# A two-layer decoder on one core: expert weight rows fetched by broadcast transfers, semaphores cleared earlier, and a GELU in halves

## The reference, cut to what matters

```python
x = x + L0_attn(layernorm(x))          # stage A, 16 heads of 64, scores refined by a small MLP
x = x + L0_xattn(layernorm(x), ctx)    # stage B
x = x + L0_ffn(layernorm(x))           # stage C
x = x + L1_attn(layernorm(x))          # stage D
x = x + L1_xattn(layernorm(x), ctx)    # stage E, masked
x = x + L1_ffn(layernorm(x))           # stage F, mixture of experts
```

```python
combined = concat([scores, kerple])                 # per query and key: 32 values
hdn = gelu(combined @ w1 + b1, approximate=False)
scores = scores + kerple + (hdn @ w2 + b2)          # then causal softmax, values, output product
```

```python
g = silu(h @ w_gate[e].T); u = h @ w_up[e].T        # h: 512 tokens x 256, 128 hidden features
routed = sum_e (g * u * combine[:, e]) @ w_down[e].T
out = routed + shared(h)
```

## Time and profile before

| | us |
|---|---|
| median of three runs (4124.12 to 4130.19) | 4125.24 |
| the profiled execution's own time | 4128.32 |
| its span, first to last instruction | 4126.5 |
| L1232 PE, x1088, mean of one | 0.598 |
| L1245 PE, x128, median of one | 0.382 |
| L1682 ACT, GELU of 128x2048, median of one | 1.97 |
| DVE idle ahead of L1716, behind L1584 | 218.7 |

### The profile page before, as it was taken

How to read it: one execution, slowest core, us unless ns; L and a number is a source line. 1 busy time by engine, 2 the same in 40 slices (tenths; PEclk the granted TensorE clock), 3 DMA queues, 4 the chain that set the end, 5 groups by cost and what they waited for, 6 DMA issues and landing times.

```text
span 4126.5 us, 59377 instructions
## 1 busy us (share of the span) xinstructions
PE 3815.9 (92%) x22610; PEld 1837.7 (45%) x22610; DVE 2427.9 (59%) x6081; ACT 1740.2 (42%) x3188; POOL 152.0 (4%) x168
## 2 busy tenths in 40 slices
PE   4899899999989989999998998999999999899999
PEld 2353444345435244435543524443553443444355
DVE  5568576832466856673236676766323776676542
ACT  1655434521274643362127464336113836433511
POOL 1000020000000002000000001100000000200000
PEclk9999999999999999999999999999999999999999
DMA  5313002122331200203242210120325121012031
GB/s 174 122 43 63 19 18 54 22 96 73 102 109 43 55 19 25 57 12 104 72 127 93 43 38 18 45 48 1 115 62 162 63 51 26 19 45 48 1 126 55
DMA packets 135286, 254.49 MB, mean 62 GB/s; under 512 B 23332, under 2 KB 82724, under 8 KB 130084
## 3 DMA queue, kind: packets, MB, share of 16 engines
q1 hardware_dynamic: 134984, 250.50, 21.7%
HBM read 156.04 MB, written 44.04 MB: 48 GB/s over the span
## 4 chain that ended last, share of the span: by engine, by line
PE 74%; DVE 16%; ACT 7%; issue 2%; PEldq 0%; SPq 0%; DMA 0%; PEld 0%; DVEq 0%; POOLq 0%; ACTq 0%
PE ps L1232 11%; PE ps L588 7%; PE ps L571 6%; PE ps L1250 5%; DVE mx L754 4%; PE ps L411 4%; PE ps L515 4%; PE ps L1604 3%; PE ps L1520 3%; PE ps L576 3%; ACT a_X L1682 2%; PE ps L467 2%; PE ps L1544 2%; DVE ps L751 2%; PE ps L1563 2%
## 5 line engine op out<-in xcount | busy, mean ns | idle before, releaser
L692 ACT ACTIVATE PT<-ps 128x512 f32<-128x512 f32 (+2 forms) x1280 | 644.2, 564 | 325.2 <-PE ps L576 174.7
L1232 PE MATMUL ps<-xnT,f_w 128*128 128x512 f32 x1088 | 493.8, 598 | 0.0
L754 DVE TENSOR_REDUCE mx<-ps 128x1 f32<-128x512 f32 (+3 forms) x768 | 431.1, 618 | 76.4 <-PE ps L515 39.6
L571 PE MATMUL ps<-QS,KS 99*128 99x512 bf16 (+2 forms) x1280 | 419.1, 369 | 8.5 <-ACT PT L692 8.0
L515 PE MATMUL ps<-KS,QS 96*128 96x512 bf16 (+3 forms) x1280 | 392.2, 368 | 17.4 <-DVE mx L754 6.9
L751 DVE CUSTOM_DVE_ANT_0 ps<-ps,mneg 128x512 f32<-128x512 f32 x512 | 340.8, 718 | 82.0 <-PE ps L515 78.9
L1338 DVE TENSOR_TENSOR f_tm<-f_si,ps 128x512 f32<-128x512 f32 x128 | 88.1, 688 | 492.1 <-ACT f_si L1290 492.0
L588 PE MATMUL ps<-PT,VP 128*32 128x512 f32 (+3 forms) x2560 | 372.0, 573 | 0.0
L411 PE MATMUL ps<-mneg,identb 128*128 128x512 bf16 x1192 | 312.9, 389 | 28.5 <-DVE a_fin L1716 10.5
L1290 ACT ACTIVATE f_si<-ps 128x512 f32<-128x512 f32 x136 | 80.8, 597 | 595.5 <-PE ps L1245 576.4
L1232 PEld LDWEIGHTS ps<-xnT,f_w 128*128 128x128 f32 x1088 | 208.6, 193 | 206.5 <-issue 199.9
(11 more groups left out here) (278 smaller groups left out, 5524.1 us busy)
## 6 DMA issues: line engine op xcount, KB each, us to landing
f_w<-in_wF SPq DMA_DIRECT2D x136, 384.0 KB, 3.1
scores<-a_fin SPq DMA_DIRECT2D x64, 256.0 KB, 3.0
a_fin<-scores SPq DMA_DIRECT2D x32, 512.0 KB, 4.5
a_Y<-in_wA SPq DMA_DIRECT2D x5, 3072.0 KB, 15.1
KS<-KP SPq DMA_DIRECT2D x240, 64.0 KB, 2.3
scores<-a_fin SPq DMA_DIRECT2D x64, 192.0 KB, 2.9
a_fin<-scores SPq DMA_DIRECT2D x12, 1024.0 KB, 7.6
a_fin<-scores SPq DMA_DIRECT2D x16, 768.0 KB, 4.3
```

What stands on the lines that cost most here:

```text
L571: last = nc.tensor.matmul(o, m["KS"][0:KST, h, j * P:(j + 1) * P], m["QS"][0:KST, h, q0:S], start=True, stop=plain)
L692: nc.scalar.activation(m["PT"][:, mp % 2, j % 2, e, 0:w], ps[:, SLOTS + n % TURNED, 0:w], ACT.Exp, scale=HD ** -0.5).then_inc(g("exp"), 1)
L754: nc.vector.tensor_reduce(m["mx"][:, h % 2, i, f // BANK:f // BANK + 1], ps[:, k % SLOTS, 0:w], AX.X, ALU.max, negate=True).then_inc(g("sl ...
L1232: last = nc.tensor.matmul(ps[:, 2 * v + e % 2, :], m["w"][:, e % NRING, (2 * v + k) * P:(2 * v + k + 1) * P], xnT[:, k, :], start=(k == 0) ...
```

## The change

Three parts. **Rows of weights.** `routed(e)` remains for e = 2 and 3 (`F_DIRECT`). For the other 30 a new product `all_rows` brings all 32 rows out once, as 32 partitions of 512 tokens; ACT copies them to `f_rows` (`rows_up`), SP stores them in DRAM (`weight_rows`, 64 KB) and then fetches row after row, each broadcast to 128 partitions (2 KB each, 256 KB together), into four slots in `ctxT`, two experts behind the transfers of expert weights on the same queue. DVE's second product reads the row there. The transposition of the weights moves into the middle of up(3). **Border.** SP clears most semaphores ahead of F's barrier, issues `out<-x` behind the second barrier instead of ahead of it, and `WARM_CLEAR` is 8. **GELU in halves.** In the 16 units of two-unit chunks the GELU is two instructions of two banks each. In the second unit of such a chunk, up(k) starts with four of its products behind the first half.

```diff
-WARM_ROUND, WARM_CLEAR = 12, 6
+WARM_ROUND, WARM_CLEAR = 12, 8
+F_ROWS = 4
+        row_in = [setup_loaded, setup_dve, setup_pool_sem, setup_act]
+        F_DIRECT = [NSH, NSH + 1]
+        rows_kept = nc.dram_tensor("weight_rows", (NE, S), F32, kind="Internal").ap()
+        def row_of(e):
+            return ctxT[:, e % F_ROWS // 2, e % 2 * S:(e % 2 + 1) * S]
@@ f_sp
+            def load_row(e):
+                if e > F_DIRECT[-1] + F_ROWS:
+                    sp.wait_ge(sm["F", "gu"], e - F_ROWS + 1)
+                sp.dma_start(row_of(e), rows_kept[e - NSH:e - NSH + 1, :].partition_broadcast(P)).then_inc(row_in[e % F_ROWS], 16)
+            lag = 2
+            first = F_DIRECT[-1] + 1
             for e in range(NE + NSH):
+                if e == first + lag + F_ROWS - 2:
+                    sp.wait_ge(sm["F", "rows_up"], 1)
+                    sp.dma_start(rows_kept, MF["rows"][:, :]).then_inc(sm["F", "rows_out"], 16)
+                    sp.wait_ge(sm["F", "rows_out"], 16)
+                    load_row(first)
+                    load_row(first + 1)
                 if e >= NRING:
                     sp.wait_ge(sm["F", "down"], e - NRING + 1)
                 sp.dma_start(MF["w"][:, e % NRING, :], io["wF"][e]).then_inc(w_in[e % NRING], 16)
...
+                if e >= first + lag + F_ROWS - 2:
+                    load_row(e - lag)
+            for e in range(NE + NSH - lag, NE + NSH):
+                load_row(e)
@@ f_pe
+                half_up(e, 0)
+                if e == F_DIRECT[-1]:
+                    weights_turned()
+                half_up(e, 1).then_inc(g("gu_mm"), 1)
...
+            def all_rows():
+                nc.tensor.matmul(ps[0:NE, 5, :], selE[:, :, 0], m["cT"][:, :], start=True, stop=True).then_inc(g("rows_mm"), 1)
...
             up(NSH + 1)
+            pe.wait_ge(g("ct_up"), 1)
             routed(NSH)
-            routed(NSH + 1)
+            all_rows()
             down(NSH)
...
-                routed(e)
+                if e - 1 in F_DIRECT:
+                    pe.wait_ge(g("rows_up"), 1)
+                    routed(e - 1)
                 down(e - 1)
@@ f_dve
+                    if e in F_DIRECT:
+                        dve.wait_ge(g("row_mm"), e - NSH + 1)
+                        row = ps[:, 4 + e % 2, :]
+                    else:
+                        dve.wait_ge(row_in[e % F_ROWS], 16 * ((e - F_DIRECT[-1] - 1) // F_ROWS + 1))
+                        row = row_of(e)
+                    nc.vector.tensor_tensor(m["gu"][:, e % 2, :], m["tm"][:, :], row, ALU.mult).then_inc(g("gu"), 1)
@@ a_pe
+                tiles = list(itertools.product(range(4), range(2)))
+                if k == FIRST[c]:
...
+                else:
+                    pe.wait_ge(g("gelu"), HIDDEN_TO[k] - 1)
+                    for e, b in tiles[:4]:
+                        scored(e, b)
+                    pe.wait_ge(g("gelu"), HIDDEN_TO[k])
+                    for (e, b), (e2, b2) in zip(tiles[:4], tiles[4:]):
+                        scored(e2, b2)
+                        last = distant(e, b, 0)
+                    last.then_inc(g("w1"), 1)
+                    for e, b in tiles[4:]:
+                        last = distant(e, b, 0)
+                    last.then_inc(g("w1"), 1)
@@ a_act
-                act.wait_ge(g("w1"), k + 1)
                 if k >= 2:
                     act.wait_ge(g("w2"), k - 1)
-                nc.scalar.activation(m["hid"][k % 2][:, :, 0:w], ps[:, A_UP:A_UP + 4, 0:w], ACT.Gelu, bias=b1A[:, 0:1]).then_inc(g("gelu"), 1)
+                n = 4 // HALVES[k]
+                for x in range(HALVES[k]):
+                    act.wait_ge(g("w1"), HIDDEN_TO[k] + x + 1)
+                    nc.scalar.activation(m["hid"][k % 2][:, n * x:n * x + n, 0:w], ps[:, A_UP + n * x:A_UP + n * x + n, 0:w], ACT.Gelu,
+                                         bias=b1A[:, 0:1]).then_inc(g("gelu"), 1)
@@ sync
+                    if s == STAGES[-1]:
+                        clear_all(sp, done_by_now)
                     st.end()
...
+                st.end_round([s for s in counting if s not in done_by_now])
                 sp.dma_start(out[bass.ds(b, 1), :, :].rearrange("o (t p) d -> p (o t) d", p=P), x[:, :, :]).then_inc(x_stored, 16)
-                st.end_round(counting)
```

More of the change, by code:

```diff
@@ L1191, in f_mem @@
             m["cT"] = sb2("f_cT", [96, S], BF16)
+            m["rows"] = sb2("f_rows", [NE, S])
             m["si"] = sb2("f_si", [P, 2, S])
@@ L1224, in f_pe, with half_up @@
             last.then_inc(g("lg_mm"), 1)
+            def half_up(e, v):
+                for k in range(KD):
+                    last = nc.tensor.matmul(ps[:, 2 * v + e % 2, :], m["w"][:, e % NRING, (2 * v + k) * P:(2 * v + k + 1) * P],
+                                            xnT[:, k, :], start=(k == 0), stop=(k == KD - 1))
+                return last
             def up(e):
@@ L1427, in decoder @@
         TILE_END = {i: max(n for n in range(NCHUNK) if CHUNKS[n][0] == i) for i in range(NI)}
+        HALVES = [2 if FIRST[c] != LAST[c] else 1 for c, _ in A_UNITS]
+        HIDDEN_TO = [sum(HALVES[:k]) for k in range(NU + 1)]
         V_HEADS = [4, 2, 1, 1]
@@ L1556, in up, with scored @@
                     pe.wait_ge(g(loaded(c)), 16 if c >= SMALL else 16 * (c // 4 + 1))
-                if k:
-                    pe.wait_ge(g("gelu"), k)
-                for e in range(4):
+                def scored(e, b):
                     rows = slice(32 * e, 32 * e + 32)
-                    for b in range(2):
-                        first = (q0 + b * R) * L
-                        nc.tensor.matmul(ps[64 * b:64 * b + 64, A_UP + e, 0:R * L], w1A[rows, 0, :], fin(c)[rows, first:first + R * L],
-                                         start=True, stop=False, tile_position=(32 * e, 64 * b), skip_group_check=True)
@@ L1565, in up @@
-                for q in range(R):
-                    for e in range(4):
-                        rows = slice(32 * e, 32 * e + 32)
-                        for b in range(2):
-                            t0 = BACK - i * P - AU * (r + q0 + b * R + q)
-                            last = nc.tensor.matmul(ps[64 * b:64 * b + 64, A_UP + e, q * L:(q + 1) * L], w1A[rows, 1, :], kerA[rows, t0:t0 + L],
-                                                    start=False, stop=True, tile_position=(32 * e, 64 * b), skip_group_check=True)
@@ L1577, in down @@
                 w = SA_R[i] * L
-                pe.wait_ge(g("gelu"), k + 1)
+                pe.wait_ge(g("gelu"), HIDDEN_TO[k + 1])
                 if k:
@@ L1911, in _ @@
             st.end_round(counting)
+            done_by_now = [ctx_loaded, *x_biased.values(), *w_loaded.values(), *(a for (stage, _), a in sm.items() if stage != STAGES[-1])]
             with sp.Fori(0, rounds) as b:
```

46 lines of the change are left out of this document (29 added, 17 removed).

## The result

Time after: 4089.64 us median of four executions (4084.67 to 4095.34), before 4124.68 (4123.81 to 4130.19); ratio 0.9913, 95% interval [0.9896, 0.993]. The forecast was 4082.5, in a range of 4068 to 4098. The profiled executions stand at 4128.32 and 4084.67, 43.6 apart against 42.7 in the sum; the medians are only 35.0 apart. The profiled execution after was the fastest of the four, and its mean granted clock was 0.987 against 0.984 to 0.985 in the others. Both have to be explained, the 43.6 and the 8 or so that the medians lack. The latter are hardly clear of noise: as a ratio the forecast was 0.9898, just inside the measured interval. The median also lies above the forecast's own range of 4076 to 4088, where rivals (a) and (b) had put theirs (4090.5 and 4089), so the number alone doesn't tell which mechanism held.

The account below looks back on a forecast made before the run. PE was taken to bound the kernel, with 74% of the chain. Stage F -39.1, stage A -6.8, border +1.3 and program's end +1.9 sum to -42.7 us, giving 4082.5 us, range 4068 to 4098.

Parts of the forecast that it names:

- (a): F's start: the clock stays low, giving back 4 x 2.0 us, 4090.5 in all; chance 0.13.
- (b): Stage A gives nothing, extra batches and DVE waits take all: 4089, or 4093 with a loss; chance 0.15.
- 29 products at 0.22: Stage F, steady part: experts 5 to 33 lose their row product on PE, 6.4 us a round.
- (d): Stage F: the row broadcast is served at the upper bound of 8.8 us, about 4470 in all; chance 0.04.
- down(2) starts at 898.29 ... 1.73 and 3.43 lead to 903.45: F's start: down(2) after 0.55 of waiting, then down and up; part of a 3.4 us gain a round.
- the 0.83 that the prediction gave to the slow clock at down(2): F's start: down(2) took 2.56 instead of 1.73 at the low clock; full clock was assumed after the change.
- 1.7 a round: Stage A: net gain of halved GELUs after the cost of extra batches, 6.8 us in all.
- The half GELU's 1.11: Stage A: a half GELU takes 1.11 us by slope, two in a row 0.14 more than the whole.
- the last two second units cost 0.7 each: Stage A: second units 13 and 15 lie where PE bounds, so each extra batch costs 0.7 us.
- -1.5 to +2: Border: range in us, each, for the change in the unexplained 3.87 us way back to the loop's head.
- (c): Stage A or border does better: way back shorter by 1.5 or batches of four overlap; about 4072, chance 0.16.
- it was 3.1 slower than the median ... against that I forecast: Whole kernel: profiled execution 4128.3 was 3.1 above the median 4125.2, so 4085.6 there became 4082.5 us.

Follow-up runs that it names:

- e4_fill: Changed kernel with two idle products ahead of down(2) and three ahead of down(3) at F's start; 4090.5 us, ratio to before 0.9907.
- e5_border_6: Kernel before with semaphores cleared earlier and the store of out behind the second barrier, idle products still six; 4135.8 us, ratio 1.0022.
- e10_whole_late: Changed kernel with the border of before and a whole GELU and one batch of eight in second units from 12 on; 4086.1 us, ratio to before 0.9902.
- e2_halves: Kernel before with only the GELU in halves, stage F and border unchanged; 4123.9 us, ratio 0.9991.
- e6_only_8: Kernel before with eight idle products at the border instead of six and nothing else; 4136.3 us, ratio 1.0023.
- e3_border: Kernel before with only the border changed: earlier clears, store of out behind the second barrier, eight idle products; 4140.3 us, ratio 1.0029.

## Why the prediction was right, and where it was not

**F, steady: right in mechanism and size.** 29 products at 0.22 were 6.38 a round, 25.5 in all. The broadcast landed after 3.4 us, beside the 3.1 taken from the expert transfer, and rival (d) was not near: its limit was put where row and expert transfer together exceed 5.16 us, and two rows with an expert's weights still did not. Issue to landing is not service time; the earlier trace rows had said so with their 1.0 us between two landings.

**F, start: the step "down(2) starts at 898.29 ... 1.73 and 3.43 lead to 903.45" was short.** It gave 2.66 a round instead of 3.4. Both waits were near the forecast, but a down behind a wait for its own stationary operand takes 1.99, not 1.73: in the steady part the first weight load starts 0.43 us ahead of its product, under the up, behind a wait it starts together with it. Twice 0.26, and 0.2 in the hand-overs. Rival (a) is refuted: 1.00 in the earlier trace rows's place after, 13.27 in all rounds of the seven other kernels profiled with this order, and no effect of `e4_fill`. The old order's low clock was in turn no certainty: in 2 of the 20 rounds profiled with it up(3) to up(5) took 14.23, not 15.93, as in round 2 of `e5_border_6`:

```profile
1911.60:1916.60 5.00, 3.09 (x12) 2.01 (x11) 2.75 (x4) 1.08 (x2) 0.00 (x0) 1.00 0.00 0
1916.60:1921.60 5.00, 5.00 (x18) 2.98 (x17) 1.28 (x2) 0.60 (x1) 0.00 (x0) 1.00 0.26 79
```

The chain of that round has the same down(2) and up(4), for the 2.56 and 4.56 of the earlier trace rows:

```profile
1913.92 1.99 PE ps L1250 x8
1915.91 3.43 PE ps L1232 x8
```

So 0.26 of the 0.83 that the prediction gave to the slow clock at down(2) were the bare weight load, which stayed. The clock was worth 1.7 of the 2.66, and the new order 0.96.

**A: 1.7 a round was near, by two errors.** The half GELU's 1.11 was right (1106 ns). Of the gains, up(5) is 1.9 earlier behind the first up and up(11) 2.9. But "the last two second units cost 0.7 each" was wrong: `e10_whole_late` finds at most 0.15. That a split up costs so little I put down to its middle, where products of both halves stand in turn; no run tested that. Up to the weighted sums 139 us behind the first up the gain is 2.3. Then half of it goes in 5 us, by the clock: the windows there after and, at the same instructions, before:

```profile
1272.20:1277.20 5.00, 5.00 (x19) 3.93 (x20) 2.46 (x10) 0.00 (x0) 0.00 (x0) 0.74 0.13 51
```
```profile
1289.90:1294.90 5.00, 4.93 (x28) 3.96 (x30) 3.24 (x13) 0.00 (x0) 0.00 (x0) 1.00 0.15 61
```

This low is no accident of one round: the six us from 136 us behind the first up ran at 0.72 to 0.75 in all 36 rounds with halves, and at 1.00 in the seven rounds of 167.4 to 167.7 with a whole GELU. Rounds 2 to 4 keep 1.1; round 1 shows 5.5, because there the kernel before was 4.2 above its other rounds. Rival (b), that A gives nothing, is refuted for A itself; in the median, `e2_halves` says 2.5 us of the 6.8.

**Border: mis-sized.** The drain grew by the forecast 0.43 (1.82 for 1.39), and the way back by 0.3 (4.19 for 3.87), which was inside "-1.5 to +2". It goes with the store's new place and the earlier clears, which no run separates, and not with the idle products: three ways back took 12.5 to 13.0 us in the traces of the six kernels with the new order, `e5_border_6` and its six products among them, and 11.8 to 12.1 in the other eight, also in `e6_only_8`. The earlier clearing gave nothing, as said. The end of the program cost the 1.9. So rival (c), a shorter way back, is refuted. What the prediction had no term for is what a shift of the rounds does behind the border. It priced two idle products at 1.3; alone on the kernel before they cost 10.

**The sum for the profiled execution: near by luck.** The rows of the first table add up to -43.7 where the forecast had -42.7. F gave 3.0 less than forecast and the borders and the end cost 1.0 more; against that stand 1.9 more in A, all of it and more from one bad round of the kernel before, and 3.1 in stretches for which the forecast had nothing.

**The median: the failed step is "it was 3.1 slower than the median ... against that I forecast".** It carries a sum made for one execution over to the medians, as if the executions of both kernels stood alike in their clock. But the profiled execution before was 3.1 above its median and the one after 5.0 below. The kernel before was the steadier of the two: 18 executions of it in one comparison had quartiles 2.6 us apart. The parts measured alone are -33.1, -2.5 and +13.9, together -21.7, and the change as a whole is -35. They don't add, since each also decides where the stages behind it fall. One piece can be named: the 7.0 us that stage A lost in the trace of `e3_border` can't come back in the changed kernel, whose GELU in halves never had that loss. For the rest it is argued. The Trainium skill (TensorE: Matmul & The Clock Gate, "A second HAM failure mode: psum-queue depth-cycling") says that frequent small idles between groups of matmuls make the clock oscillate. The waits of 1.2 us ahead of 0.53 and ahead of 1.00 agree with it in part: such a wait can be followed by either. Where the changed kernel's execution of 4095.3 lost its time is open, since it has no profile; that it was in that stretch is argued from the other kernels, not shown.

## What to carry over

Price a removed matmul by what the chain counts of it and not by its duration, and give the first product behind a wait for its stationary operand its weight load as well. A row that many partitions need could here be fetched by a broadcast beside the weight stream, issued well ahead of its use, at no cost to PE; measure the margin by doubling it. Where a kernel has many waits of about 1 us, an edit of 0.4 us a round can move the whole by 10: read the untouched stretches too, with their granted clock, and compare medians of several executions before an edit of a tenth of a per cent is called good or bad.

## What the runs showed of the hardware

- The same instructions behind the same wait of 1.2 us ran at a granted clock of 1.00, 0.84 or 0.53 from round to round (22, 18 and 8 of 48), and the 0.53 cost 3.1 us there. With four idle products in the wait it was 1.00 in the eight rounds profiled.
- A DRAM row of 2 KB read by 128 partitions landed in 3.4 us, 384 KB of weights in 3.1 us, and two such rows an expert beside the weights still left PE's 5.16 us untouched.
- PE's first down behind a wait took 1.99 us, in the steady part 1.73; the first weight load then started with its product instead of 0.43 us ahead.
- An up cut into 4, 8 and 4 tiles delayed the next down by 0.12 to 0.14 us against one cut 8 and 8, where eight products alone, four side by side, had taken 0.91.
- With the 512 KB store issued behind the last barrier, and semaphores cleared earlier, three ways back to the loop's head took 12.5 to 13.0 us in sum; with the old order 11.8 to 12.1.
